# A four-block cross-attention kernel: first loads in another order and on another queue, a signal for each load, and a prologue in another order

## The reference

```python
def L0(x_c, x_s, Wn, bn, Wm, bm, Wl, bl, Wo, bo):          # over the token axis
    Mn = conv1x1(Wn, bn, inorm(x_c)); Mm = conv1x1(Wm, bm, inorm(x_s))
    A = softmax(einsum('bct,bcs->bts', Mn, Mm))
    Mo = einsum('bcs,bts->bct', conv1x1(Wl, bl, x_s), A)
    return conv1x1(Wo, bo, Mo) + x_c
def L1(x, ctx, mask, Wq, Wk, Wv, Wo, gamma, beta, gate):   # L2 is the same with its own weights
    a = layer_norm(ctx, gamma, beta)
    Q, K, V = x @ Wq.T, a @ Wk.T, a @ Wv.T                 # 16 heads of 16
    P = softmax(where(mask, Q K^T / 4, -inf))
    return x + tanh(gate) * (P V) @ Wo.T
def L3(x, ctx, w_q, w_k, w_v, w_o, alpha):                 # one head of 256
    P = softmax((x @ w_q.T) (ctx @ w_k.T)^T / 16)
    return x + alpha * (P (ctx @ w_v.T)) @ w_o.T
x = L0(x, ctx); x = L1(x, ctx, mask); x = L2(x, ctx, mask); x = L3(x, ctx)
```

## Time and profile before

| | |
|---|---|
| median of 3 runs | 611.54 us (609.24 to 611.83) |
| the profiled execution | 612.3 us, of which the span from first to last instruction is 610.5 us |
| busy | PE 568.1 us, DVE 469.9, ACT 468.9, POOL 118.2 |
| mean granted TensorE clock | 0.991 |
| moved by DMA | 18.32 MB, 8.5% of the 16 engines' time on SyncE's queue |

### The profile page before, as it was taken

How to read it: one execution, slowest core, us unless ns; L and a number is a source line. 1 busy time by engine, 2 the same in 40 slices (tenths; PEclk the granted TensorE clock), 3 DMA queues, 4 the chain that set the end, 5 groups by cost and what they waited for, 6 DMA issues and landing times.

```text
span 610.5 us, 25738 instructions
## 1 busy us (share of the span) xinstructions
PE 568.1 (93%) x10867; PEld 499.8 (82%) x10867; DVE 469.9 (77%) x1023; ACT 468.9 (77%) x961; POOL 118.2 (19%) x132
## 2 busy tenths in 40 slices
PE   1799999999999999999999999999999999999885
PEld 1678888988798887988889887998889887988774
DVE  5775879787887869778796869878797869876653
ACT  0799879878787779877788769867788778878651
POOL 3603070103310070102501061100601052000000
PEclk9999999999999999999999999999999999999988
DMA  5520001110020100210020100210020100010001
GB/s 144 174 76 2 2 3 45 35 37 2 2 75 3 37 2 4 75 37 2 2 76 2 38 2 3 75 37 2 3 76 2 37 2 3 3 35 4 2 3 34
DMA packets 18500, 18.32 MB, mean 30 GB/s; under 512 B 1829, under 2 KB 18341, under 8 KB 18405
## 3 DMA queue, kind: packets, MB, share of 16 engines
q1 hardware_dynamic: 18024, 16.55, 8.5%
q0 software_dynamic: 320, 0.26, 0.2%
q10 hardware_dynamic: 60, 0.01, 0.0%
HBM read 12.63 MB, written 4.19 MB: 28 GB/s over the span
## 4 chain that ended last, share of the span: by engine, by line
PE 70%; DVE 11%; ACT 10%; issue 5%; DMA 1%; SPq 1%; POOL 0%; DVEq 0%; ACTq 0%; POOLq 0%
PE psum L389 10%; PE psum L728 10%; PE psum L674 9%; PE psum L390 8%; PE psum L391 8%; PE psum L721 5%; DVE negmax L1048 4%; ACT work L849 4%; PE psum L641 4%; PE psum L654 3%; PE psum L544 3%; DVE shifted L1052 2%; ACT v L800 2%; PE psum L453 2%; PE psum L552 1%
## 5 line engine op out<-in xcount | busy, mean ns | idle before, releaser
L849 ACT ACTIVATE work<-shifted 128x512 f32<-128x512 f32 x128 | 79.2, 632 | 19.0 <-DVE shifted L1052 18.5
L1048 DVE TENSOR_REDUCE negmax<-psum 128x8 f32<-128x512 f32 x128 | 87.2, 681 | 7.1 <-PE psum L654 7.1
L1052 DVE TENSOR_TENSOR shifted<-psum,negmax 128x512 f32<-128x512 f32 x128 | 88.5, 691 | 5.2
L863 ACT ACTIVATE work<-psum,group_mask 128x512 f32<-128x512 f32 x128 | 80.5, 697 | 12.6 <-PE psum L674 12.6
L674 PE MATMUL psum<-const,work 64*128 64x64 f32 x1536 | 64.2, 228 | 17.9 <-ACT work L849 14.6
L674 PEld LDWEIGHTS psum<-const,work 64*128 64x128 f32 x1536 | 54.4, 140 | 32.2 <-ACT work L849 20.0
L728 PEld LDWEIGHTS psum<-v,work 128*64 128x64 f32 x2048 | 63.9, 141 | 8.0 <-issue 5.9
L728 PE MATMUL psum<-v,work 128*64 128x34 f32 x2048 | 67.5, 227 | 0.0
L844 ACT ACTIVATE work<-psum,negmax 128x256 f32<-128x256 f32 x128 | 50.3, 512 | 11.4 <-DVE negmax L1044 11.4
L800 ACT ACTIVATE v<-psum 64x256 f32<-64x256 f32 x128 | 49.8, 389 | 11.3 <-PE psum L391 10.0
L792 ACT ACTIVATE kbd<-psum,own_bias,const 128x512 f32<-128x512 f32 x64 | 46.3, 778 | 4.7 <-PE psum L391 4.4
(11 more groups left out here) (181 smaller groups left out, 1536.8 us busy)
## 6 DMA issues: line engine op xcount, KB each, us to landing
x_raw<-in_x_dram SPq DMA_DIRECT2D x8, 512.0 KB, 4.3
c_raw<-in_ctx_dram SPq DMA_DIRECT2D x8, 512.0 KB, 5.0
out_dram<-attn SPq DMA_DIRECT2D x16, 256.0 KB, 2.3
mrow_u<-in_mask_dram SPq DMA_DIRECT2D x8, 64.0 KB, 4.9
kbd<-in_L_xattn_Wq_dram SPq DMA_DIRECT2D x2, 256.0 KB, 6.8
kbd<-in_L_xattn_Wk_dram SPq DMA_DIRECT2D x2, 256.0 KB, 7.1
kbd<-in_L_xattn_Wv_dram SPq DMA_DIRECT2D x2, 256.0 KB, 7.3
kbd<-in_L_xattn_Wo_dram SPq DMA_DIRECT2D x2, 256.0 KB, 8.2
```

The lines of the kernel that those rows point to most:

```text
L849: act.activation(probs[:, exp_row(g, l, i, last), :], shifted[:, i % 4, :], ACT.Exp).then_inc(exps, 1)
L863: act.activation(probsT[:, at, :], o[:], ACT.Copy, scale=group_mask[:, 2 * i + c:2 * i + c + 1]).then_inc(free, 1)
L1048: dve.tensor_reduce(negmax[:, i % 2, :], sv, AX_X, ALU.max, negate=True).then_inc(rowmax, 1)
L1052: dve.tensor_tensor(shifted[:, i % 4, :].rearrange("t (j k) -> t j k", k=C), sv, negmax[:, i % 2, :].unsqueeze(2).broadcast_to([P, NJ, C]) ...
```

## The change

SyncE issues x_raw and c_raw first, then w0, the mask rows, bo, and the weights of blocks 1, 2 and 3. It no longer waits for w0 and L0's biases in between. The const load goes to ScalarE's queue, ahead of the mask. group_loaded becomes x_loaded, c_loaded and rows_loaded: TensorE's xT, cT and V0 and VectorE's statistics wait for the load that they read, GpSimd's front for the mask rows alone; the turning of the first x and context waits for const as well. A statistics step takes two pairs of one input, where it took one pair of each: ST.0 and ST.1 are x, ST.2 and ST.3 the context. The three prologue orders are rewritten. The orders of a pass stay.

```diff
 PE_FIRST = """
-    MT.0 W0T.0 GT.0 MS.0 cT.0-1 xT.0-1 W0.0 Wq1.0 Wk1.0 Wo1.0 Wq2.0 V0.0-1 Wv1.0 Wk2.0 Mn.0-1 Mm.0-1 Wo3T.0 nT.0-1 VW3.0
-    S0.0-3 M3.0 T0.0-1 S0.4-5 T0.2-3 S0.6-7 A0.0 Wv2.0 A0.1-3 T0.4-5 Wo2.0 VB1.0 T0.6-7 A0.4 K1.0 A0.5 K1.1 VB2.0 A0.6-7
-    Q1.0
+    MT.0 MS.0 xT.0-1 cT.0-1 GT.0 Wq1.0 Wk1.0 Wv1.0 W0T.0 nT.0-1 Wq2.0 Wv2.0 Mn.0-1 Wk2.0 W0.0 Mm.0-1 Wo3T.0 V0.0-1 S0.0-3
+    VB1.0 S0.4-5 T0.0-1 S0.6-7 M3.0 T0.2-3 VW3.0 A0.0-1 T0.4-5 A0.2-3 T0.6-7 A0.4-5 Wo1.0 Wo2.0 K1.0-1 VB2.0 A0.6-7 Q1.0
 """
 ACT_FIRST = """
-    cT.0 xT.0-1 cT.1 Wq1.0 Wk1.0 NM.1 NM.0 TG.0 Wo1.0 Wq2.0 Wv1.0 Wk2.0 Mn.0-1 Mm.0-1 Wo3T.0 nT.0-1 KB.1 VW3.0 X0.0-2 M3.0
-    X0.3 T0.0-1 X0.4 T0.2-3 X0.5 Wv2.0 X0.6-7 T0.4 VB1.0 T0.5 Wo2.0 KB.2 T0.6-7 H.0 K1.0 VB2.0 OB.1 Q1.0 K1.1 H.1 OB.2
+    xT.0-1 cT.0-1 Wq1.0 Wk1.0 Wv1.0 NM.1 NM.0 TG.0 nT.0-1 Wq2.0 Wv2.0 Mn.0 Wk2.0 Mn.1 Mm.0-1 Wo3T.0 KB.1 X0.0-4 T0.0 VB1.0
+    T0.1 X0.5-6 OB.1 M3.0 X0.7 T0.2-3 VW3.0 T0.4-5 KB.2 Wo1.0 Wo2.0 T0.6-7 H.0 K1.0 VB2.0 K1.1 Q1.0 H.1 OB.2
 """
 DVE_FIRST = """
-    MT.0 WB.0 ON.0 MS.0 ST.0 W0T.0 GT.0 ST.1-2 TG.0 ST.3 MV.0 NB.0 Wq1.0 cT.0-1 W0.0 Wk1.0 Wo1.0 Wq2.0 Wv1.0 V0.0-1 Wk2.0
-    Mn.0-1 Mm.0-1 nT.0 S0.0 nT.1 S0.1-2 VW3.0 S0.3 M3.0 S0.4-7 Wv2.0 A0.1 A0.3 Wo2.0 L.0 A0.5 A0.7 L.1
+    ST.0 MT.0 ST.1-2 MS.0 ST.3 GT.0 MV.0 ON.0 cT.0 NB.0 WB.0 Wq1.0 cT.1 Wv1.0 TG.0 Wk1.0 W0T.0 nT.0-1 Wq2.0 W0.0 Mn.0
+    Wv2.0 Mn.1 Mm.0-1 Wk2.0 V0.0 S0.0-3 V0.1 S0.4-7 A0.1 M3.0 VW3.0 A0.3 A0.5 Wo1.0 Wo2.0 L.0 A0.7 L.1
 """
...
             def load_group(g):
-                sp.dma_start(x_raw[:], x_g[g]).then_inc(group_loaded, 16)
-                sp.dma_start(c_raw[:], c_g[g]).then_inc(group_loaded, 16)
+                sp.dma_start(x_raw[:], x_g[g]).then_inc(x_loaded, 16)
+                sp.dma_start(c_raw[:], c_g[g]).then_inc(c_loaded, 16)
                 sp.dma_start(mrow_u8[:].rearrange("r p k -> r (p k)"),
-                             m_g[g].unsqueeze(0).broadcast_to([P, TOK])).then_inc(group_loaded, 16)
+                             m_g[g].unsqueeze(0).broadcast_to([P, TOK])).then_inc(rows_loaded, 16)
...
-            sp.dma_start(const[:], cst).then_inc(const_loaded, 16)
+            sp.dma_start(x_raw[:], x_g[0]).then_inc(x_loaded, 16)
+            sp.dma_start(c_raw[:], c_g[0]).then_inc(c_loaded, 16)
             for i, n in enumerate(("Wn", "Wm", "Wo", "Wl")):
                 sp.dma_start(w0_raw[:, i, :], w[f"L0_xattn_{n}"].unsqueeze(0).broadcast_to([2, C, C])).then_inc(w0_loaded, 16)
-            load_group(0)
-            sp.wait_ge(w0_bias_loaded, 3 * 16)
-            sp.wait_ge(w0_loaded, 4 * 16)
+            sp.dma_start(mrow_u8[:].rearrange("r p k -> r (p k)"),
+                         m_g[0].unsqueeze(0).broadcast_to([P, TOK])).then_inc(rows_loaded, 16)
+            sp.dma_start(bo_row, w["L0_xattn_bo"].unsqueeze(0).broadcast_to([P, C])).then_inc(bo_loaded, 16)
             for n in "qkvo":
                 sp.dma_start(raw[n + "1"][:], w_in(w[f"L1_xattn_W{n}"])).then_inc(w1_loaded, 16)
-            sp.dma_start(bo_row, w["L0_xattn_bo"].unsqueeze(0).broadcast_to([P, C])).then_inc(bo_loaded, 16)
...
             def front_halves(g, name, banks, signals):
 
-                if name == "xT" and g is not None:
-                    pe.wait_ge(group_loaded, g * 48 + 96)
+                pe.wait_ge(x_loaded if name == "xT" else c_loaded, 16 if g is None else g * 16 + 32)
+                if g is None:
+                    pe.wait_ge(const_loaded, 16)
...
-                if g is None and name in ("xT", "cT", "V0"):
-                    pe.wait_ge(group_loaded, 48)
+                if name == "V0":
+                    pe.wait_ge(c_loaded, 16 if g is None else g * 16 + 32)
...
+            act.dma_start(const[:], cst).then_inc(const_loaded, 16)
             act.dma_start(mask_u8[:], mask.rearrange("(p h) s -> p (h s)", h=2)).then_inc(mask_loaded, 16)
...
-            def stats_step(g, p):
-
-                if p == 0:
-                    dve.wait_ge(group_loaded, 48 if g is None else 48 * g + 96)
-                for t, src in ((p, x_raw), (NP + p, c_raw)):
-                    ins = dve.bn_stats(stats[:, t, :], src[:, p, :])
+            def stats_step(g, n):
+
+                src, at = ((x_raw, 0), (c_raw, NP))[n // 2]
+                if n % 2 == 0:
+                    dve.wait_ge((x_loaded, c_loaded)[n // 2], 16 if g is None else 16 * g + 32)
+                for p in (2 * (n % 2), 2 * (n % 2) + 1):
+                    ins = dve.bn_stats(stats[:, at + p, :], src[:, p, :])
                 ins.then_inc(stats_ready, 1)
...
-                hold(group_loaded, 48 * nth)
+                hold(rows_loaded, 16 * nth)
```

More of the change, by code:

```diff
@@ L299, in build @@
         gates_loaded, gates_spread, gamma_loaded = sem("gates_loaded"), sem("gates_spread"), sem("gamma_loaded")
-        group_loaded = sem("group_loaded")
+        x_loaded, c_loaded, rows_loaded = sem("x_loaded"), sem("c_loaded"), sem("rows_loaded")
         cleared, w0_ready = sem("cleared"), sem("w0_ready")
```

## The result

The changed kernel takes 613.20 us in the median of 20 runs (611.04 to 616.36); the kernel before, run beside it, 611.38 (609.24 to 613.39, 20 runs). The ratio is 1.0033, with a 95% interval of 1.0020 to 1.0045: 1.8 us slower. That is less than the 0.5% of the chances, so it counts as "same" there, but it is on the other side of no change, and 0.2 us above the range of 606.5 to 613.0. The profiled execution has a span of 612.9 us against 610.5.

A forecast was written before the change was run, and what follows sets the result against it. Passes being dense, only an earlier start of the first pass counts: 5.4 us won on statistics and 3.7 on w1 shrink to 1.3 at V1.0, plus 0.6 for S1's vanished wait, so 611.54 - 1.9 = 609.6 us; range 606.5 to 613.0.

The forecast's parts named there:

- The walk from w1's landing to S1: Prologue: 4.0 us earlier at NM.0, 3.3 at S0, 1.3 at V1.0, S1 at 55.4 instead of 57.29.
- the sum for w1's landing: Prologue loads: w1 lands at 14.7 us (13.5 to 16) instead of 18.4, a gain of 3.7.
- The last issue: SyncE's queue: w1's last part is issued near 9.2 us, where it was 9.69.
- Rival C: Prologue loads: w1 lands no sooner than about 17.5, crowded by x, c and w0; 611 to 612 us; chance 0.16.
- A second term of the sum: ScalarE's queue: mask behind const lands at about 3.3 us; VectorE's start chain ends at 8.1, not 7.7.
- the shift of S1: First S1 matmul after the prologue: its move from 57.29 to 55.4 was taken as the whole gain, 1.9 us.
- The gap ahead of nT: TensorE in the prologue: idle about 2 us, from 18.6 to 20.6, waiting for NM.1.
- S0 to V1.0: TensorE late in the prologue: 21.86 us instead of 19.87, as VW3 adds 1.99.
- Rival B: Prologue: ScalarE alone bounds, the waits at W0 and S0.1 vanish; 4.4 us less, 607.1; chance 0.24.
- Rival D: TensorE in the prologue: its fast pace comes later than about 34 us; slower, 614.6 us; chance 0.10.
- The const move: Const load to ScalarE's queue: by the skill's rule gains nothing and may delay x by 0.4 us, inside the slack.
- The forecast of 609.6: Whole kernel: median 611.54 less 1.9 us gained in the prologue; chance 0.50.

The follow-up runs named there:

- c3: Changed kernel with the two beta loads moved from GpSimd's queue to SyncE behind w1; 610.26 us in one execution.
- a3: Changed kernel with the four w0 broadcast loads issued as eight plain loads of 64 partitions; 613.89 us, ratio 1.0064 to the kernel before.
- a4: Changed kernel with the mask issued ahead of const on ScalarE's queue; 613.66 us, ratio 1.0035 to the kernel before.
- d1: Changed kernel with w1 ahead of mask rows, w0 and bias row, mask ahead of const, beta loads behind the bias row on SyncE; 608.34 us, ratio 0.9952.
- c4: Changed kernel with w1's loads ahead of mask rows, w0 and bias row on SyncE's queue; 610.76 us, ratio 0.9996 to the kernel before.
- a1: Changed kernel's loads and signals with the three prologue orders of the kernel before; 612.01 us, ratio 1.0026 to the kernel before.
- b4: Changed kernel with only the mask rows and bias row moved to ScalarE's queue, w0 left ahead of w1 on SyncE; 613.44 us in one execution.
- c2: Changed kernel with the four w0 loads put back ahead of x_raw and c_raw on SyncE's queue; 614.01 us in one execution.

## Why the prediction was wrong

The walk from w1's landing to S1 held, from mark to mark; its starting point, when w1 lands, was wrong.

- **The step that failed** is the sum for w1's landing: "then the small w0 loads (131 KB, at that row's 36 GB/s 3.6 us, but beside others), mask rows, bias, and 1 MB of w1 ...: 13.5 to 16. I take 14.7". w1 landed at 19.2 and its first transpose came at 19.36, 4.7 us later than the sum and 3.4 above its upper end. Three terms were too small. First, the slow rate of the earlier trace rows was applied to w0 alone. All 224 KB of w0, mask rows and bias together went at about that rate: with the beta loads out of the way (c3) the stretch ahead of w1 carries 35 GB/s. Second, the two beta loads stand in the "about 2.7 MB" but have no time of their own in the sum. They are half of the bytes in the slow stretch, and moving them away brings w1 1.8 us sooner (one execution). Together the stretch lasts 6.7 us, from 6.8 to 13.5, where the sum leaves 4 to 5 of the 8.2 between 6.5 and 14.7. Third, from its first packet at 13.5 to its landing w1 takes 5.7 us, where 1 MB at the 240 to 340 GB/s of the sum takes 3.1 to 4.4. The first parts of w2 land at 17.8, before the last of w1; why w1's last parts come so late is not shown. The last issue, put at 9.2, was at 12.17, but a3 shows that this was not what counted: there it was at 9.91 and w1 came no sooner. Rival C named this mechanism (landing after 17.5, broadcast loads as slow in the middle of the queue) and got 0.16. Its price, 611 to 612, was too low in part because 17.5 was its landing and not 19.2.
- **A second term of the sum**, smaller: "it landed after 2.1 us, so at about 3.3 now". Behind const and with x already flowing the mask took 5.3 us, the cast came at 6.51, and VectorE's start chain ended at 11.4 instead of 8.1. norm_bias came at 19.67, where its end was predicted at 17.1. With the mask ahead of const (a4) the cast is at 3.86; by itself that is worth nothing, in d1 it is part of the gain.
- **A mark that was chosen wrongly.** I took the shift of S1 for the gain. But the loop was entered 1.34 us after S1 in the kernel before (57.29, 58.63) and 0.68 us after it in the changed one (58.71, 59.39); c4 and d1 have 0.69 and 0.68. So S1 at 55.4 would have been worth 2.6 us and not 1.9. In the changed kernel this is why 1.4 us lost at S1 are only 0.8 at the loop.
- **What held.** c4 is the nearest to what I assumed: w1's first transpose at 14.27 (14.7), S0 at 32.37 (31.95), S1 at 55.48 (55.4). In the changed kernel: from w1's first transpose to S0 17.25 predicted, 16.28 measured. The gap ahead of nT: 2 predicted, 1.80. S0 stands for the bank of Wk2's copy: the trace has 1.64 <-DVE wT_k_lo. S0 to V1.0: 21.86 predicted, 21.56. S0 to S1: 23.45 predicted, 23.07, and the wait for K1's copy gone. The passes unchanged: 486.2 us against 486.0 for seven. Two sums are off by little: VectorE's steps from 8.1 add up to 13.5 and not 13.7, and 27.2 + 4.8 is 32.0.
- **Rival B** is not borne out: in c4, with w1 early, TensorE still waits 1.64 us at S0, and S1 is at 55.48, not before 54.
- **Rival D** did not happen: W0's 16 matmuls at 28.64 take 1.09 us, so the fast pace had come by then, before the 34 us from which it would decide. But its reading of the clock column was wrong. The 1.00 of the earlier trace rows and of the windows above is printed where the trace has no record of the clock: the records start at 29.57 us in the kernel before and at 28.19 in the changed one. Where there are records, the pace follows them. In a1 the 64 matmuls of V0 (L481) take 218 ns each until 26.2 and 311 from 26.4 on, and the record falls from 1.00 to 0.50 at 26.32, after TensorE had been busy 0.66 of the 2.7 us from 22.9:

```profile
25.60:26.30 0.70, 0.59 (x39) 0.59 (x43) 0.70 (x3) 0.70 (x2) 0.70 (x2) 1.00 0.00 0
26.40:29.70 3.30, 3.30 (x49) 2.67 (x44) 1.30 (x5) 3.27 (x9) 0.66 (x1) 0.50 0.02 5
```

In d1 nT's take 311 at a recorded 0.50, the 1.2 GHz level, and V0's 218 at 1.00, the 2.4 GHz level. So the early pace is the lower level, as rival D supposed. This is what it took from the Trainium skill (TensorE: Matmul & The Clock Gate, What's actually happening), by which the clock is halved by default, and the traces agree.
- **The const move**, against which the prediction itself spoke, saved SyncE an issue of 0.4 us and cost the mask 2.7 (landed at 6.49, in a4 at 3.84).

The forecast of 609.6 is bracketed by the kernels with w1 early: 610.76 for c4, 1.2 above, and 608.34 for d1, 1.3 below, which has the mask ahead and the beta loads behind as well.

## What to carry over

Before a prologue is reordered, add up the small loads (broadcast rows, half-size weights) at the rate that the trace shows for them, those of other engines' queues too, and treat this sum as serial: here everything issued behind them landed that much later, with the DMA engines mostly idle. Put large loads that are wanted early ahead of the small ones, leave the smallest and most urgent at the head of its own queue, and look at how long an issue takes before you give it to an engine that has to compute soon. An order of steps and an order of loads are one design: each of the two halves here lost by itself, and the new orders are worth nothing with the loads of the change (1.0033 against 1.0026) and 0.75% with loads that suit them (0.9952 against 1.0027).

## What the runs showed of the hardware

**The issue of a small load can hold its engine for microseconds while earlier loads are on their way.** The same 32 KB load of w0 (Wo) took 2.81 us to issue on SyncE in the changed kernel, 5.12 with w1 ahead, 2.77 with w1 ahead and beta behind, and 6.21 on ScalarE; in the loop an issue of 512 KB takes 0.39. It ended at 6.98, 12.20 and 9.70 us on SyncE, shortly before the last landing of loads issued ahead of it (c_raw at 7.65, the mask rows at 12.34, w1 at 9.91). That it waits for these is likely, but no run varies this alone.

**GpSimd can slow VectorE down.** norm_bias, an instruction on 128x8 numbers, takes 1.23 us where GpSimd starts its product of a weight just before it (21.30 in the kernel before, 19.67 in the changed one, 18.44 in c4) and 0.17 where GpSimd stands still (18.05 in b4, 17.30 in c2, 16.20 in d1).

**The end of the kernel scatters by its granted clock.** From the eighth group mask to the end, window of each (columns as in the earlier trace rows), in the kernel before, the changed one, b4, c4 and d1:

```profile
544.67:610.50 65.83, 53.92 (x894) 47.34 (x894) 39.49 (x79) 36.98 (x73) 0.00 (x0) 0.92 0.06 18
```

```profile
545.61:612.90 67.29, 55.49 (x894) 48.66 (x894) 39.52 (x79) 37.02 (x73) 0.00 (x0) 0.89 0.05 18
```

```profile
548.22:611.60 63.38, 51.44 (x894) 44.75 (x894) 39.45 (x79) 36.93 (x73) 0.00 (x0) 0.95 0.06 19
```

```profile
542.04:609.30 67.26, 55.54 (x894) 48.73 (x894) 39.50 (x79) 37.00 (x73) 0.00 (x0) 0.89 0.06 18
```

```profile
541.23:606.20 64.97, 52.74 (x894) 46.48 (x894) 39.49 (x79) 36.91 (x73) 0.00 (x0) 0.93 0.06 18
```

The work is the same to the instruction, VectorE and ScalarE are busy equally long, and the stretch lasts 63.4 us at a mean granted clock of 0.95 and 67.3 at 0.89; in slices of five us it falls to 0.50, the 1.2 GHz level (590 to 595 in the kernel before, 595 to 600 in the changed one). The eleven other traces lie between 63.9 and 67.4. So 1.5 of the 2.4 us between the two profiled executions are of this kind. Whether the changed kernel falls lower more often, which would make the missing 1.0 us between its entry (0.8) and its median (1.8), or whether that is elsewhere in the runs without a profile, stays open.
